# Attention with the denominators' product from summed key tiles, four buffers of probabilities, and half of the value projection moved ahead of the first values

## The chip, the cores and the metric

One core of a Trainium2 chip runs one program. The metric is the device time of one execution in microseconds, lower is better.

## The reference

The input is 16 sequences of 256 tokens with 256 channels, float32. Three stages are added to it in turn: half of a mixture-of-experts layer, attention, and half of the same expert layer again. Only the attention bears on this change:

```python
q = (X @ Wq).reshape(b, t, 16, 32).transpose(0, 2, 1, 3)     # 16 heads of 32
k, v = ...                                                    # 8 key/value heads of 32
q = q * cos + _rotate_half(q) * sin                           # the same for k
k, v = jnp.repeat(k, 2, axis=1), jnp.repeat(v, 2, axis=1)
att = 50.0 * jnp.tanh(einsum('bhqd,bhkd->bhqk', q, k) * 256.0 ** -0.5 / 50.0)
att = jnp.where(causal, att, -jnp.inf)
y = einsum('bhqk,bhkd->bhqd', softmax(att), v)
return y.transpose(0, 2, 1, 3).reshape(b, t, 512) @ Wo
```

X is layer-normalised before, and the result is added to the stage's input.

## The kernel before

The program runs the first expert layer, the attention, and the second expert layer one behind the other. The attention (function `attention`) takes one sequence of 256 tokens a slot, 16 slots. Each engine has its own instruction order, written out by hand in a function `slot_of`, and the engines meet on semaphores. For sequences 1 to 12 TensorE runs a loop whose body holds two slots; the rest is written out. The slots overlap three sequences: in the slot of sequence b TensorE also works on the projections of b + 1, the transposes of b + 2 and the last values and output product of b - 1.

A sequence has two groups (g) of four key/value heads, and two tiles (t) of 128 keys; a unit u = 2g + t is one group with one key tile. For a unit:

- `score_unit` makes the transposed scores, keys in the partitions: four heads, for each the two query heads that share it. Key tile 0 has all 256 queries (512 columns a head), key tile 1 only the later 128 (256 columns a head), since the earlier ones do not see those keys.
- ScalarE makes tanh (`cap`, tile `capped`) and the exponential (`exponential`, tile `probs`), each 128x2048 or 128x1024.
- GpSimd zeroes what is above the diagonal in the first 128 queries of the unit (`causal`), in place in `probs`, and counts `probs_ready`.
- `weighted_values` makes two products, each with 4 heads, 32 output partitions a head: `den`, with weights of ones (`m.ones_f`), so that each of the 32 partitions of a head holds the sum over keys, and `pv`, with the values `v`. Both add over the two key tiles in PSUM. In float32 each call shows as two instructions in the trace, so that a bank of four heads is eight.

`probs` has two buffers, by u % 2. After both tiles of a group VectorE's `invert` transposes `den` (32x32 blocks), takes reciprocals of one column of each block and transposes back, ScalarE's `take_values` copies `pv` to SBUF, and `divide` multiplies the two to `y`. `output` multiplies `y` with Wo into the bank `pj[0]`, and `residual` adds it to the input. `project(b, q, n)` has four pieces: n = 0 to 2 are chunks of queries and keys, which VectorE's `turn` reads (product with cos, and a shuffle to `turned`) and GpSimd's `rope` finishes (product with sin, sum); n = 3 is the value projection, copied by ScalarE (`copy_v`). Each piece is 12 matmuls of 256 columns, in a split of high and low parts (`split_matmul`). `PIECE_BANK = (1, 0, 0, 1)`: piece 3 goes into the bank that piece 0 had, so it waits for the first turn. `aT_lo_part` and `aT_hi_part` make the low and high part of the transposed input that the projections read; GpSimd's `root` and VectorE's `statistics` belong to the layer norm of b + 2.

GpSimd's order in a slot is causal 0, rope, causal 1, rope, root, causal 2, rope, causal 3.

Of the kernel before, what the change touches and what calls it, by code (L numbers as in the profile page):

```python
# [18 lines left out]
P = 128  # L19
# [1265 lines left out]
def attention(nc, m, src, dst, front):  # L1285

    ctx = ExitStack()
    with ctx:
# [35 lines left out]
        probs = sb("probs", [P, 2, JH, W], F32)  # L1324
# [33 lines left out]
        pv_done = sem("pv_done")  # L1358
        taken = sem("taken")
# [39 lines left out]
        def _(pe):  # L1399
# [9 lines left out]
            def project(b, q, n):  # L1409
# [7 lines left out]
                for c in range(2):  # L1417
# [9 lines left out]
                last.then_inc(piece_ready, 1)  # L1427
# [15 lines left out]
            def weighted_values(b, q, u):  # L1443
                g, t = u // QT, u % QT
                pe.wait_ge(probs_ready, b * UNITS + u + 1)
                if t == 0:
                    at_least(pe, taken, b * GROUPS + g)
                    at_least(pe, den_taken, b * GROUPS + g)
                n = REP * (SEQ - t * P)
                for bank, ones in ((den, True), (pv, False)):  # L1450
                    for j in range(JH):
                        w = m.ones_f[:] if ones else v[:, q, t, (JH * g + j) * HD:(JH * g + j + 1) * HD]
                        out = bank[j * HD:(j + 1) * HD, :].rearrange("p (r s) -> p r s", r=REP)[:, :, t * P:SEQ]
                        last = nc.tensor.matmul(out, w, probs[:, u % 2, j, 0:n].rearrange("p (r s) -> p r s", r=REP),  # L1454
                                                start=t == 0, stop=t == QT - 1)
                last.then_inc(pv_done, 1)
# [13 lines left out]
            def slot_of(b, q, behind=True, ahead=True, further=True):  # L1470

                score_unit(b, q, 0)
                if behind:
                    weighted_values(b - 1, 1 - q, 3)
                if ahead:
                    project(b + 1, 1 - q, 0)
                    project(b + 1, 1 - q, 1)
                score_unit(b, q, 1)
                weighted_values(b, q, 0)
                score_unit(b, q, 2)  # L1480
                if ahead:
                    project(b + 1, 1 - q, 2)
                    project(b + 1, 1 - q, 3)
                weighted_values(b, q, 1)
                score_unit(b, q, 3)
                if behind:
                    output(b - 1)
                weighted_values(b, q, 2)
# [14 lines left out]
            weighted_values(SEQS - 1, 1, 3)  # L1503
            output(SEQS - 1)

        @block.scalar
        def _(act):
# [25 lines left out]
            def exponential(b, u):  # L1533

                act.wait_ge(capped_ready, b * UNITS + u + 1)
                at_least(act, pv_done, b * UNITS + max(u - 1, 0))
                n = REP * (SEQ - u % QT * P)
                nc.scalar.activation(probs[:, u % 2, :, 0:n], capped[:, u % 2, :, 0:n], ACT.Exp,  # L1538
# [41 lines left out]
        def _(pool):  # L1580
# [17 lines left out]
            def causal(b, u):  # L1598
# [3 lines left out]
                diag = probs[:, u % 2, :, 0:n].rearrange("p j (r s) -> p j r s", r=REP)[:, :, :, 0:P]  # L1602
# [33 lines left out]
        def _(dve):  # L1636
# [26 lines left out]

            def invert(b, g):
                n = b * GROUPS + g
                dve.wait_ge(pv_done, b * UNITS + QT * (g + 1))
# [16 lines left out]
            def slot_of(b):  # L1683
# [12 lines left out]
                invert(b, 0)  # L1696
                if behind:
                    residual(b - 1)
                divide(b, 0)
                if further:  # L1700
                    aT_lo_part(b + 2)

# [96 lines left out]
```

## Time and profile before

| | |
|---|---|
| median of 3 runs | 1027.0 us (1026.89 to 1028.26) |
| the profiled execution's own time | 1027.73 us |
| its span | 1026.0 us |
| attention in the span, first scores to last residual | 366.5 to 695.1 us |
| one slot in the steady part | 20.23 us |
| TensorE's granted clock over the span | 0.979 of full speed |

The span is from the first to the last instruction of the profiled execution; its own time is a little longer, and sums are made against that. Line numbers, as L1454, are lines of the kernel before. In the trace PE is TensorE, DVE VectorE, ACT ScalarE, POOL GpSimd. A row of a tile names the tile written, an arrow and the tiles read; the tiles of the attention end in _at. Line 80 to 82 is `split_matmul`, 1438 the scores, 1454 the products of `weighted_values`, 1467 `output`, 1603 `causal`, 1594 and 1596 `rope`, 1667 to 1671 `invert`, 1677 `divide`, 1662 the shuffle of `turn`.

### The profile page before, as it was taken

The page shows a single profiled execution, that of the slowest core. Times are in us where ns is not written, and L with a number is a line of the kernel's source. Part 1 is how long each engine was busy: PE and PEld are TensorE (multiplying, and loading weights), DVE is VectorE, ACT ScalarE, POOL GpSimd, SP SyncE. Part 2 cuts the span into 40 slices and gives each one's busy share as a digit, 9 for nine tenths or more (in the row PEclk, how much of TensorE's full clock was granted, in tenths as well). Part 3 has the DMA queues.
Part 4 walks back from the last instruction along what each step waited for, and adds up shares of the span by engine and source line. Part 5 has one row for each costly group of instructions (what it writes and reads, how often), then busy time and mean ns, then how long its engine had stood idle before and what let it go on. Part 6 is the DMA issues. An engine that isn't in the chain of part 4 may idle for free. (4 is left out here: it accounts for less than half of the span.)

```text
span 1026.0 us, 17887 instructions
## 1 busy us (share of the span) xinstructions
PE 939.1 (92%) x6146; PEld 694.0 (68%) x6146; DVE 626.0 (61%) x1637; ACT 521.2 (51%) x765; POOL 472.7 (46%) x534
## 2 busy tenths in 40 slices
PE   2999998999999489999999999977999989999997
PEld 1788876777778456565666556635888767777786
DVE  4888777544444456665665676545988776453435
ACT  3766742132233257776777677655676622231322
POOL 5333203556542075776577567613512224555640
PEclk9999999999999799999999999988999999999999
DMA  5434235778774300000100100013323265777835
GB/s 186 118 96 126 67 95 150 172 179 184 174 172 104 123 1 22 21 21 31 31 20 21 41 20 21 11 62 94 94 84 111 68 175 133 170 182 180 181 58 170
DMA packets 95432, 101.90 MB, mean 99 GB/s; under 512 B 18688, under 2 KB 86656, under 8 KB 95360
## 3 DMA queue, kind: packets, MB, share of 16 engines
q1 hardware_dynamic: 83072, 83.17, 27.0%
q0 software_dynamic: 12288, 17.83, 10.4%
q8 instruction: 37, 0.61, 0.2%
q14 instruction: 35, 0.29, 0.1%
HBM read 65.44 MB, written 35.54 MB: 98 GB/s over the span
## 5 line engine op out<-in xcount | busy, mean ns | idle before, releaser
L80 PE MATMUL gu<-x_hi,gu_hi 128*128 128x512 f32 x308 | 139.9, 454 | 4.8 <-DVE act_gu L1124 4.8
L82 PE MATMUL gu<-x_lo,gu_hi 128*128 128x512 f32 x308 | 123.1, 400 | 0.0
L81 PE MATMUL gu<-x_hi,gu_lo 128*128 128x512 f32 x308 | 122.5, 398 | 0.0
L1603 POOL TENSOR_SCALAR_AFFINE_SELECT probs_at<-probs_at 128x1024 f32<-128x1024 f32 x64 | 70.5, 1102 | 110.8 <-ACT probs_at L1538 110.8
L1530 ACT ACTIVATE capped_at<-scores_at 128x2048 f32<-128x2048 f32 x64 | 93.1, 1454 | 45.1 <-PE scores_at L1438 44.9
L671 POOL DMA_INDIRECT rows<-z_rows,slots x64 | 68.9, 1077 | 75.4 <-DVE slots L1115 56.5
L957 ACT CAST a_hi<-act_gu 128x512 fp32r<-128x512 f32 x96 | 59.2, 616 | 83.1 <-DVE act_gu L1124 62.2
L1538 ACT ACTIVATE probs_at<-capped_at 128x2048 f32<-128x2048 f32 x64 | 95.2, 1487 | 2.0
L80 PE MATMUL down<-down_hi,a_hi 128*128 128x256 f32 x300 | 93.7, 312 | 0.2 <-DVE a_lo L1134 0.2
L867 PE MATMUL zT<-w_gu,xT 128*128 128x352 f32 x256 | 86.3, 460 | 0.0
L1005 ACT ACTIVATE y<-gu,rows 128x256 f32<-128x256 f32 x64 | 30.3, 474 | 109.9 <-PE gu L887 95.9
L81 PE MATMUL down<-down_hi,a_lo 128*128 128x256 f32 x300 | 83.7, 279 | 0.0
L82 PE MATMUL down<-down_lo,a_hi 128*128 128x256 f32 x300 | 83.7, 279 | 0.0
L679 POOL DMA_INDIRECT acc<-y,slots x32 | 51.1, 1597 | 70.5 <-DMA acc<-y,slots 58.6
L679 POOL DMA_INDIRECT out<-y,slots x32 | 51.3, 1604 | 69.9 <-DMA out<-y,slots 55.4
L258 POOL TENSOR_TENSOR rstd_f<-var_in_f,neg_half 128x8 f32<-128x8 f32 x16 | 26.7, 1670 | 120.6 <-DVE var_in_f L253 120.6
L949 ACT ACTIVATE silu<-gu 128x512 f32<-128x512 f32 x80 | 47.6, 596 | 61.6 <-PE gu L82 58.3
L1239 DVE TENSOR_SCALAR xT<-zT,w_norm_pairs 128x128 f32<-128x128 f32 x128 | 39.0, 346 | 62.4 <-PE zT L858 47.7
L80 PEld LDWEIGHTS gu<-x_hi,gu_hi 128*128 128x128 f32 x308 | 59.0, 192 | 21.8 <-DVE act_gu L1124 6.9
L887 PE MATMUL gu<-w_down,prodT 88*128 88x256 f32 x256 | 70.7, 399 | 0.5 <-issue 0.5
L1454 PE MATMUL den_at<-probs_at,ones_f 128*32 128x256 f32 (+1 forms) x512 | 55.4, 504 | 14.8 <-POOL probs_at L1603 14.8
L1596 POOL TENSOR_TENSOR roped_at<-by_cos_at,by_sin_at 128x512 f32<-128x512 f32 x48 | 66.4, 1383 | 3.8
(220 smaller groups left out, 2403.3 us busy)
## 6 DMA issues: line engine op xcount, KB each, us to landing
w_gu<-in_w_gate SPq DMA_DIRECT2D x64, 176.0 KB
w_gu<-in_w_up SPq DMA_DIRECT2D x64, 176.0 KB
w_down<-in_w_down SPq DMA_DIRECT2D x64, 176.0 KB
z_rows<-z SPq DMA_DIRECT2D x16, 512.0 KB, 3.1
acc<-base SPq DMA_DIRECT2D x10, 512.0 KB, 3.6
out<-base SPq DMA_DIRECT2D x10, 512.0 KB, 4.0
x_f<-in_X SPq DMA_DIRECT2D x8, 512.0 KB, 4.7
xn_at<-acc SPq DMA_DIRECT2D x16, 256.0 KB, 2.8
```

Source lines behind the costliest of these rows:

```text
L80: nc.tensor.matmul(out, w_hi, x_hi, start=first, stop=False)
L81: nc.tensor.matmul(out, w_lo, x_hi, start=False, stop=False)
L82: return nc.tensor.matmul(out, w_hi, x_lo, start=False, stop=last)
L671: pool.indirect_dma_start(out=gathered_rows[:, n, :], out_offset=None, in_=m.z_rows, in_offset=bass.IndirectOffsetOnAxis(ap=slots[:, e:e + ...
L679: pool.indirect_dma_start(out=acc, out_offset=bass.IndirectOffsetOnAxis(ap=slots[:, e:e + 1], axis=0), in_=y[:, e % HELD_Y, :], in_offset= ...
L867: last = nc.tensor.matmul(gu_ps, xT[:, e % 2, k, :], w_gu[:, n, :, k, :], start=k == 0, stop=k == KC - 1)
L887: last = nc.tensor.matmul(y_ps, prodT[:, e % 2, k, :], w_down[:, n, k, :], start=k == 0, stop=k == 1)
L957: nc.scalar.copy(a_hi[rows_, mt, :], act_gu[rows_, mt % 2, :]).then_inc(a_hi_ready, 1)
L1530: nc.scalar.activation(capped[:, u % 2, :, 0:n], scores[:, :, 0:n], ACT.Tanh, scale=QK_SCALE / SOFTCAP).then_inc(capped_ready, 1)
L1538: nc.scalar.activation(probs[:, u % 2, :, 0:n], capped[:, u % 2, :, 0:n], ACT.Exp, scale=SOFTCAP).then_inc(exp_ready, 1)
L1596: pool.tensor_tensor(roped[:, q, c:c + 2, :], by_cos[:, n], by_sin[:, n], ALU.add).then_inc(roped_ready, 1)
L1603: pool.affine_select(out=diag, in_=diag, compare_op=ALU.is_ge, fill=zero, base=0, pattern=[[0, JH], [0, REP], [1, P]], channel_multiplier= ...
```

## The change

- `probs` has four buffers, one a unit. The exponential of unit u now waits for the denominators (`den_done`) of the same group one sequence earlier, where it waited for the values of the unit two before.
- The denominators leave `weighted_values`, which keeps the product with the values. A new `denominators(b, g)` on TensorE makes, for the first 128 queries, the ones product of key tile 0 alone, and for the later 128 the ones product of a tile `both`; each is 256 columns a head and neither adds in PSUM.
- A new `add_tiles(b, g)` on VectorE makes `both`: key tile 0's later 128 queries plus key tile 1, 4 heads x 2 x 128 columns, 128x1024 in float32. It waits for the masks of both units and for the denominators that read this buffer a sequence ago. `denominators` waits for it (`summed`), and `invert` for `denominators`.
- On TensorE `denominators(b - 1, 1)` stands behind the last values of b - 1, `denominators(b, 0)` between `output(b - 1)` and the third values.
- The value projection of b + 1 is cut in two halves of 128 tokens, six matmuls each; the first goes between the scores of unit 1 and the values of unit 0, the second stays.
- On VectorE `add_tiles(b, 0)` stands behind the third turn and ahead of the residual, `invert(b, 0)` moves behind the residual, then come `add_tiles(b, 1)`, `aT_lo_part(b + 2)` and, now last, `divide(b, 0)`.

```diff
--- before.py
+++ after.py
@@ -1321,7 +1321,8 @@
         roped = sb("roped", [P, 2, 6, SEQ], F32)
         v = sb("v", [P, 2, QT, C], F32)
         capped = sb("capped", [P, 2, JH, W], F32)
-        probs = sb("probs", [P, 2, JH, W], F32)
+        probs = sb("probs", [P, UNITS, JH, W], F32)
+        both = sb("both", [P, GROUPS, JH, REP, P], F32)
         pv_sb = sb("pv_sb", [P, GROUPS, W], F32)
         BLOCKS = W // HD
         den_T = sb("den_T", [P, BLOCKS, HD], F32)
@@ -1356,6 +1357,8 @@
         exp_ready = sem("exp_ready")
         probs_ready = sem("probs_ready")
         pv_done = sem("pv_done")
+        summed = sem("summed")
+        den_done = sem("den_done")
         taken = sem("taken")
         den_taken = sem("den_taken")
         inv_T_ready = sem("inv_T_ready")
@@ -1406,7 +1409,7 @@
                         last = nc.tensor.transpose(pj[0][:, k, t * P:(t + 1) * P], a[:, t, k * P:(k + 1) * P], m.ident[:])
                 last.then_inc(aT_ready, 1)
 
-            def project(b, q, n):
+            def project(b, q, n, halves=(0, 1)):
 
                 bank = pj[PIECE_BANK[n]]
                 if n == 0:
@@ -1414,7 +1417,7 @@
                     pe.wait_ge(aT_lo_ready, b + 1)
                 elif n >= 2:
                     pe.wait_ge(turned_ready, b * PIECES + (2 if n == 2 else 1))
-                for c in range(2):
+                for c in halves:
                     for k in range(KC):
                         if n < PIECES:
                             chunk = 2 * ((n - 1) % PIECES) + c
@@ -1424,7 +1427,8 @@
                             at = slice(c * P, (c + 1) * P)
                             last = split_matmul(nc, bank[:, c, :], aT_hi[:, k, at], aT_lo[:, k, at],
                                                 m.v_hi[:, k, :], m.v_lo[:, k, :], k == 0, k == KC - 1)
-                last.then_inc(piece_ready, 1)
+                if halves[-1] == 1:
+                    last.then_inc(piece_ready, 1)
 
             def score_unit(b, q, u):
                 g, t = u // QT, u % QT
@@ -1445,15 +1449,28 @@
                 pe.wait_ge(probs_ready, b * UNITS + u + 1)
                 if t == 0:
                     at_least(pe, taken, b * GROUPS + g)
-                    at_least(pe, den_taken, b * GROUPS + g)
                 n = REP * (SEQ - t * P)
-                for bank, ones in ((den, True), (pv, False)):
+                for j in range(JH):
+                    w = v[:, q, t, (JH * g + j) * HD:(JH * g + j + 1) * HD]
+                    out = pv[j * HD:(j + 1) * HD, :].rearrange("p (r s) -> p r s", r=REP)[:, :, t * P:SEQ]
+                    last = nc.tensor.matmul(out, w, probs[:, u, j, 0:n].rearrange("p (r s) -> p r s", r=REP),
+                                            start=t == 0, stop=t == QT - 1)
+                last.then_inc(pv_done, 1)
+
+            def denominators(b, g):
+
+                pe.wait_ge(summed, b * GROUPS + g + 1)
+                at_least(pe, den_taken, b * GROUPS + g)
+                for of_both in (False, True):
                     for j in range(JH):
-                        w = m.ones_f[:] if ones else v[:, q, t, (JH * g + j) * HD:(JH * g + j + 1) * HD]
-                        out = bank[j * HD:(j + 1) * HD, :].rearrange("p (r s) -> p r s", r=REP)[:, :, t * P:SEQ]
-                        last = nc.tensor.matmul(out, w, probs[:, u % 2, j, 0:n].rearrange("p (r s) -> p r s", r=REP),
-                                                start=t == 0, stop=t == QT - 1)
-                last.then_inc(pv_done, 1)
+                        if of_both:
+                            weights = both[:, g, j]
+                        else:
+                            weights = probs[:, QT * g, j].rearrange("p (r s) -> p r s", r=REP)[:, :, 0:P]
+                        at = slice(of_both * P, (of_both + 1) * P)
+                        out = den[j * HD:(j + 1) * HD, :].rearrange("p (r s) -> p r s", r=REP)[:, :, at]
+                        last = nc.tensor.matmul(out, m.ones_f[:], weights, start=True, stop=True)
+                last.then_inc(den_done, 1)
 
             def output(b):
                 pe.wait_ge(y_ready, b * GROUPS + GROUPS)
@@ -1472,19 +1489,23 @@
                 score_unit(b, q, 0)
                 if behind:
                     weighted_values(b - 1, 1 - q, 3)
+                    denominators(b - 1, 1)
                 if ahead:
                     project(b + 1, 1 - q, 0)
                     project(b + 1, 1 - q, 1)
                 score_unit(b, q, 1)
+                if ahead:
+                    project(b + 1, 1 - q, 3, (0,))
                 weighted_values(b, q, 0)
                 score_unit(b, q, 2)
                 if ahead:
                     project(b + 1, 1 - q, 2)
-                    project(b + 1, 1 - q, 3)
+                    project(b + 1, 1 - q, 3, (1,))
                 weighted_values(b, q, 1)
                 score_unit(b, q, 3)
                 if behind:
                     output(b - 1)
+                denominators(b, 0)
                 weighted_values(b, q, 2)
                 if further:
                     transposes(b + 2)
@@ -1501,6 +1522,7 @@
             slot_of(SEQS - 2, 0, further=False)
             slot_of(SEQS - 1, 1, ahead=False, further=False)
             weighted_values(SEQS - 1, 1, 3)
+            denominators(SEQS - 1, 1)
             output(SEQS - 1)
 
         @block.scalar
@@ -1533,9 +1555,9 @@
             def exponential(b, u):
 
                 act.wait_ge(capped_ready, b * UNITS + u + 1)
-                at_least(act, pv_done, b * UNITS + max(u - 1, 0))
+                at_least(act, den_done, (b - 1) * GROUPS + u // QT + 1)
                 n = REP * (SEQ - u % QT * P)
-                nc.scalar.activation(probs[:, u % 2, :, 0:n], capped[:, u % 2, :, 0:n], ACT.Exp,
+                nc.scalar.activation(probs[:, u, :, 0:n], capped[:, u % 2, :, 0:n], ACT.Exp,
                                      scale=SOFTCAP).then_inc(exp_ready, 1)
 
             def take_values(b, g):
@@ -1599,7 +1621,7 @@
 
                 wait_apart(pool, exp_ready, b * UNITS + u + 1, pool_marks)
                 n = REP * (SEQ - u % QT * P)
-                diag = probs[:, u % 2, :, 0:n].rearrange("p j (r s) -> p j r s", r=REP)[:, :, :, 0:P]
+                diag = probs[:, u, :, 0:n].rearrange("p j (r s) -> p j r s", r=REP)[:, :, :, 0:P]
                 pool.affine_select(out=diag, in_=diag, compare_op=ALU.is_ge, fill=zero, base=0,
                                    pattern=[[0, JH], [0, REP], [1, P]], channel_multiplier=-1).then_inc(probs_ready, 1)
 
@@ -1661,9 +1683,17 @@
                 dve.tensor_tensor(by_cos[:, n], bank[:], cos, ALU.mult)
                 dve.stream_shuffle(turned[:, n], bank[:], [(i + HD // 2) % HD for i in range(HD)]).then_inc(turned_ready, 1)
 
+            def add_tiles(b, g):
+
+                dve.wait_ge(probs_ready, b * UNITS + QT * (g + 1))
+                at_least(dve, den_done, (b - 1) * GROUPS + g + 1)
+                first = probs[:, QT * g].rearrange("p j (r s) -> p j r s", r=REP)[:, :, :, P:SEQ]
+                second = probs[:, QT * g + 1, :, 0:REP * P].rearrange("p j (r s) -> p j r s", r=REP)
+                dve.tensor_tensor(both[:, g], first, second, ALU.add).then_inc(summed, 1)
+
             def invert(b, g):
                 n = b * GROUPS + g
-                dve.wait_ge(pv_done, b * UNITS + QT * (g + 1))
+                dve.wait_ge(den_done, n + 1)
                 dve.transpose(den_T[:].rearrange("p n d -> p (n d)"), den[:]).then_inc(den_taken, 1)
                 dve.wait_ge(den_taken, n + 1)
                 dve.reciprocal(inv_T[:], den_T[:, :, 0]).then_inc(inv_T_ready, 1)
@@ -1693,12 +1723,14 @@
                     statistics(b + 2)
                 if ahead:
                     turn(b + 1, 2)
-                invert(b, 0)
+                add_tiles(b, 0)
                 if behind:
                     residual(b - 1)
-                divide(b, 0)
+                invert(b, 0)
+                add_tiles(b, 1)
                 if further:
                     aT_lo_part(b + 2)
+                divide(b, 0)
 
             statistics(0)
             statistics(1)
```

## Rows read from the trace of the kernel before

**Rows 1.** Page, engines' busy time over the whole span.
```profile
PE 939.1 (92%) x6146; PEld 694.0 (68%) x6146; DVE 626.0 (61%) x1637; ACT 521.2 (51%) x765; POOL 472.7 (46%) x534
```

**Rows 2.** Windows of one slot, slot 14 and slot 15: busy us (instructions), clock, DMA.
```profile
506.24:526.47 20.23, 19.46 (x165) 12.12 (x164) 13.03 (x24) 14.86 (x14) 13.28 (x13) 1.00 0.09 26
647.68:667.13 19.45, 18.88 (x161) 11.62 (x160) 10.86 (x19) 13.88 (x12) 12.24 (x10) 1.00 0.01 4
667.13:690.60 23.47, 16.39 (x132) 6.77 (x128) 8.81 (x14) 13.08 (x11) 4.41 (x4) 0.85 0.21 66
```

**Rows 3.** TensorE in order of time, slot 7, and outputs of slot 15: start, length.
```profile
506.24 1.14 PE L1438 MATMUL scores_at<-roped_at 32*128 32x512 f32 x8
...
507.31 0.64 PE L1454 MATMUL den_at<-probs_at,ones_f 128*32 128x256 f32 x8
...
508.31 0.39 PE L80 MATMUL pj_at<-aT_hi_at,qk_hi 128*128 128x256 f32 x1
...
511.31 0.71 PE L1438 MATMUL scores_at<-roped_at 32*128 32x256 f32 x8
...
512.79 1.06 PE L1454 MATMUL den_at<-probs_at,ones_f 128*32 128x512 f32 x8 [0.77 <-POOL probs_at L1603]
...
513.64 1.07 PE L1454 MATMUL pv_at<-probs_at,v_at 128*32 128x512 f32 x8
...
514.64 1.14 PE L1438 MATMUL scores_at<-roped_at 32*128 32x512 f32 x8
...
515.71 0.38 PE L80 MATMUL pj_at<-aT_hi_at,qk_hi 128*128 128x256 f32 x1
...
518.74 0.64 PE L1454 MATMUL den_at<-probs_at,ones_f 128*32 128x256 f32 x8
...
519.19 0.61 PE L1454 MATMUL pv_at<-probs_at,v_at 128*32 128x256 f32 x8
...
519.74 0.71 PE L1438 MATMUL scores_at<-roped_at 32*128 32x256 f32 x8
...
520.38 3.72 PE L1467 MATMUL pj_at<-o,y_at 128*128 128x256 f32 x16
...
524.03 1.06 PE L1454 MATMUL den_at<-probs_at,ones_f 128*32 128x512 f32 x8
...
681.58 3.72 PE L1467 MATMUL pj_at<-o,y_at 128*128 128x256 f32 x16
...
690.62 3.72 PE L1467 MATMUL pj_at<-o,y_at 128*128 128x256 f32 x16 [2.60 <-DVE y_at L1677]
```

**Rows 4.** GpSimd in order of time: the end of slot 0, and slot 7.
```profile
384.23 1.10 POOL L1603 TENSOR_SCALAR_AFFINE_SELECT probs_at<-probs_at 128x1024 f32<-128x1024 f32 x1
...
511.44 1.10 POOL L1603 TENSOR_SCALAR_AFFINE_SELECT probs_at<-probs_at 128x1024 f32<-128x1024 f32 x1 [6.64 <-ACT probs_at L1538]
...
512.51 1.28 POOL L1594 TENSOR_TENSOR by_sin_at<-turned_at,sin 128x512 f32<-128x512 f32 x1
...
513.87 1.60 POOL L1596 TENSOR_TENSOR roped_at<-by_cos_at,by_sin_at 128x512 f32<-128x512 f32 x1
...
517.86 1.30 POOL L1596 TENSOR_TENSOR roped_at<-by_cos_at,by_sin_at 128x512 f32<-128x512 f32 x1
...
523.93 1.10 POOL L1603 TENSOR_SCALAR_AFFINE_SELECT probs_at<-probs_at 128x1024 f32<-128x1024 f32 x1
```

**Rows 5.** VectorE's groups by line and form: one with 1024 elements a partition.
```profile
L1162 DVE TENSOR_TENSOR base<-base,x_f 128x1024 f32<-128x1024 f32 x4 | 4.7, 1222 | 0.1
```

**Rows 6.** VectorE in order of time, slot 7; last row: tile y_at, all 32.
```profile
508.45 0.72 DVE L1667 STREAM_TRANSPOSE den_T_at<-den_at 128x512 f32<-128x512 f32 x1 [0.71 <-PE pv_at L1454]
...
510.70 0.74 DVE L1662 STREAM_SHUFFLE turned_at<-pj_at 128x512 f32<-128x512 f32 x1
...
512.66 1.68 DVE L1677 TENSOR_TENSOR y_at<-pv_sb_at,inv_den_at 128x512 f32<-128x512 f32 x1
...
L1677 DVE TENSOR_TENSOR y_at<-pv_sb_at,inv_den_at x32: 684/1212/1693, 381.8 to 689.9; 128x512 f32<-128x512 f32 x32
```

## The prediction

> **What bounds the kernel now.** I read the page first, then a table of windows cut at the slots, the order of time of each engine in one slot, and the groups by line. The page gives TensorE 92% of the span [rows 1]. The diff touches only the attention, 16 slots of one sequence each between 366.5 and 694 us, so the next view is one slot: 20.23 us long, TensorE's matmuls busy 19.46, at the full 2.4 GHz (granted 1.00), VectorE 13.03, ScalarE 14.86, GpSimd 13.28 [rows 2]. The reader should see that TensorE is the bound and the others have 5 to 7 us of room, but that this room is not free: each of them works in a fixed order, so the place of their idle time matters.
>
> I call the stations of TensorE's slot S0 to S3 (scores), W0 to W3 (weighted values, now with denominators), P (projections), O (output), T (transposes). Their starts [rows 3] show one wait that is not work: W0 starts at 512.79, 0.77 of it waiting for GpSimd's mask, which is only done at 512.54 [rows 4]. S1 to S2 would otherwise be free at 511.31 + 0.64 (as S3 to O) = 511.95, so the hole is 0.84 us.
>
> GpSimd is the second thing to see: it starts its first mask 5.20 us after S0 (511.44 less 506.24; scores, tanh and exponential stand in front of it) and then has no idle time until its fourth mask ends at 525.03, 18.79 after S0 [rows 3, 4]. Anything that delays it in that stretch delays the fourth mask one for one.
>
> **TensorE, work removed.** A bank of four 512-wide outputs takes 0.85 us (512.79 to 513.64), of four 256-wide ones 0.45 (518.74 to 519.19) [rows 3]. Now a group's denominators are 0.85 + 0.45; afterwards two 256-wide sets, 0.90, which is 0.40 less. By width alone it would be half of 0.85, 0.43. I take 0.85 a slot for the two groups. By place: W0 loses 0.85, W1 0.45, the stretch W3 to P0 gains 0.45 (values, then two sets), the stretch O to S0 keeps its length.
>
> **TensorE, value projection.** Six of its twelve matmuls move ahead of W0. Twenty-four take 3.00 us from 508.31 to 511.31 with the changeover to scores [rows 3], so 2.80 / 24 x 6 = 0.70 for six. They leave P2's stretch and go into the 0.84 hole. They add one changeover: a stretch of matmuls followed by another kind shows about 0.2 us beyond its streaming (3.00 against 2.80). So S1 + 0.64 + 0.90 brings W0 to 7.03 after S0, plus whatever the stretch before is late; the mask is done 6.30 after S0. The hole is gone.
> The Trainium skill (TensorEngine Tiling (Array Packing), Key Properties) says that a change of tiling mode drains the engine. By that rule the extra changeover is certain; without it the slot would be 0.2 us shorter. The 0.2 of the rows agrees.
>
> Slot without any new wait: 20.23 - 0.84 - 0.85 + 0.20 = 18.74, and laid out station by station 18.71: S0 0, W3 1.07, D1 1.52, P0 2.49, S1 5.49, half projection 6.13, W0 7.03, S2 8.03, P2 9.10, W1 11.42, S3 11.97, O 12.61, D0 16.26, W2 17.15, next S0 18.71. (D0, D1 are the denominators of the two groups.)
>
> **VectorE's adds.** One add is 128x1024 in float32 from two SBUF operands: that same size takes 1.22 us [rows 5]. Two are 2.44 a slot, VectorE 13.03 to 15.5 of about 19: not a bound by its sum. The first add follows the third turn and has until O ends; covered. Its price is on GpSimd. An SBUF-by-SBUF product of 512 takes 0.68 alone and 1.69 at most; the one issued at 512.66, while GpSimd's product ran to 513.79, ended at 514.34, 0.55 behind it, and GpSimd's next product, issued at 513.87, took 1.60 where its like takes 1.30 [rows 4, 6]. So they take turns. The third turn ends 12.2 after S0; GpSimd is then in its second rope's sum, which runs to 12.9 (519.16 less 506.24 [rows 4]). The add runs 12.87 to 13.94 and GpSimd loses 1.07 less the 0.17 by which its start is hidden in the row above, 0.90. The fourth mask ends at 18.79 + 0.90 = 19.7. If nothing is shared the loss is 0, if a blocked operation gives back nothing, 1.07 or more.
> The Trainium skill (SBUF — State Buffer, Who interferes with whom) has this rule, and it speaks against the change: a VectorE instruction with two SBUF inputs and a GpSimd one that reads SBUF exclude each other for the whole instruction. By it the slot is the 19.17 that I come to below; with a fair sharing, a loss of about 0.5, it would be 19.0. The rows above agree with the lock.
>
> **The new wait, D1.** The second add can start when the fourth mask is done (19.7) and VectorE has inverted the first group: D0 16.26, 1.14 from two 256-wide banks' start to the transpose (507.31 to 508.45 [rows 3, 6]), 1.67 for the inversion gives 19.06 and what the slot is late. So the mask decides. GpSimd is idle then, the add takes 1.22, and TensorE sees it 0.05 to 0.25 later (the mask at 512.54 let W0 go at 512.79 [rows 3, 4]): D1 may start at 21.15 after its own S0. It would start at 18.71 + 1.52 = 20.23, and with a stall s in this slot and the last, 20.23 + 2s. So s = 0.46. Behind D1 in TensorE's order stand P0, P1, S1 and all else; the stall is paid in full, once a slot. Its second effect is on the inversion and first turn behind it (2.99 us from 508.45 to the shuffle's end at 511.44 [rows 6]): turned at 5.73 + s, GpSimd wants it at 6.27; covered up to s = 0.5, beyond it each us passes on to GpSimd. The shift of aT_lo behind the add and of divide(b, 0) is hidden: P0 waits for D1 longer, and O needs y a slot later.
> The exponentials' wait moves to a denominator that is long done, and before it none of them waited for a product; four buffers give nothing by themselves. More SBUF, no DMA is touched.
>
> **Sum.** Full slot 18.71 + 0.46 = 19.17, gain 1.07. Twelve of them (2 to 13): 12.8. Slots 0 and 1 together: slot 0 loses nearly 2 us, but its fourth mask ends only at 385.33 now [rows 4] and 0.9 later with an add in front, so D1 of slot 1 waits about 2.2; I take 0.55 for both (bounds -1 and 2.5). Slot 14 has neither transposes nor root: 19.45 now [rows 2], 0.87. The last slot has no projections and waits on ScalarE; some of TensorE's work there ran at 1.2 GHz (granted 0.85 on average [rows 2]); I take it that W0 did, so that its 0.85 less is worth twice that and the last slot's first O comes 1.75 earlier, but from that O to the last one are 9.04 us now (681.58 to 690.62 [rows 3]) and then O 3.65, D0 and inversion 2.80, add 1.3, D1 and inversion 2.80, divide 0.74: 11.3. Loss 0.5. 12.8 + 0.55 + 0.87 - 0.5 = 13.7. Against the profiled execution's own 1027.73: 1014.0; the median of the runs shown is 0.73 lower, so 1013.3. The expert stage behind is the same work, started earlier; I expect nothing from it.
>
> **Rivals.**
> - The adds cost GpSimd nothing (1008 to 1010). Then the D0 chain decides: add from 19.06 + s, D1 at 20.4 + s against 20.23 + 2s, s about 0.2; gain 1.3 x 12 + 1 + 1 - 0.5 = 17, 1010; with no stall at all 1.52 a slot, 1007. For it: whichever engine issues first wins, and the second rope could be through. Against: GpSimd has no gap after its first mask. Chance 0.2.
> - GpSimd sets the pace (1017 to 1022): adds block or are blocked at more places, as when the product behind the second turn also falls on a rope, and D1 is ready at 21.7: beyond s = 0.5 the lateness feeds back, 2s = 1.47 + s - 0.49, s = 0.98, gain 0.55 x 12 = 6.6, 1020. Chance 0.18.
> - The other side: the add, whose first operand is read in eight pieces, takes 2.4 us instead of 1.22. It holds GpSimd 1.2 longer and itself ends 1.2 later; D1 is ready at 23.55, s = 3.32 - 0.49 = 2.8, slot 21.5, 1.3 longer than now: about 1043. It decides from D1 ready at 22.25, that is adds of 1.77 us each. For it: so little is needed. Against: products of equal size keep 1.22 with several shapes. Chance 0.07.
> - It does nothing that can be measured (within 0.2%): stall and saving meet, adds near 1.75. Chance 0.05.
>
> **How the numbers follow.** The forecast, 1013.3 with its own range 1010 to 1017, has 0.5. For 8 in 10 I reach to the no-stall bound and to the paced case: 1006 to 1020. Within 0.2% of no change is about what a measurement of this kernel can tell. Faster 0.88, same 0.05, slower 0.07.
>
> **What would show it.** Slot length 19.2; no wait of W0 for GpSimd; D1's weight load waiting for VectorE about 0.5 us, every slot; the first add at 1.4 to 2 us, the second at 1.22; GpSimd's first rank-root operation about 0.9 later than now; fourth mask 19.7 after S0; denominators' matmuls all 256 wide. Wrong if the first add runs clear of GpSimd, if an add is over 1.7 us with GpSimd idle, or if W0 waits again.

## The result, and the profile after

The changed kernel takes 1016.8 us (median of 4 runs, 1015.4 to 1018.5) where the kernel before takes 1027.0 (1026.9 to 1028.3): ratio 0.990, 95% interval [0.988, 0.992]. That is faster by 10.2 us; 1013.3 was forecast, and the range was 1006 to 1020. The profiled execution is the fastest of the four, 1015.36 us with a span of 1013.6.

The page's line of busy time:

```profile
PE 929.7 (92%) x6146; PEld 692.1 (68%) x6146; DVE 649.0 (64%) x1669; ACT 518.0 (51%) x765; POOL 485.5 (48%) x534
```

TensorE is still at 92% of a shorter span, with 9.4 us less of matmuls; VectorE has 23 us more [rows 1]. The adds alone are more than that (24 in slots 2 to 13 at 1.37 us on average); the product to `y`, moved to another place in the order, fell from 1.27 to 0.76 us on average in the same slots. Windows cut at slots 7, 8, 14 and 15 (columns as in [rows 2]):

```profile
500.74:520.16 19.42, 18.94 (x165) 12.02 (x165) 13.40 (x27) 14.67 (x14) 14.59 (x14) 1.00 0.08 27
520.16:539.27 19.11, 18.95 (x166) 12.01 (x165) 14.84 (x27) 14.66 (x14) 14.06 (x14) 1.00 0.09 28
635.56:654.03 18.47, 18.34 (x161) 11.57 (x160) 12.16 (x20) 13.67 (x12) 12.88 (x11) 1.00 0.01 4
654.03:677.47 23.44, 15.25 (x140) 6.69 (x136) 13.33 (x21) 13.08 (x11) 4.55 (x5) 0.88 0.21 66
```

A full slot was 20.23 and is now 19.42 or 19.11, in turn. TensorE's idle time in it is 0.5 and 0.2 us where it was 0.8. From the last slot's first scores to the last output's start are 23.44 us where they were 23.49.

TensorE in order of time in slot 7 (502.93 and 522.03 are the second group's denominators, 507.58 the half projection), and the last output:

```profile
500.74 1.14 PE L1442 MATMUL scores_at<-roped_at 32*128 32x512 f32 x8
...
501.81 0.64 PE L1456 MATMUL pv_at<-probs_at,v_at 128*32 128x256 f32 x8
...
502.93 0.64 PE L1472 MATMUL den_at<-probs_at,ones_f 128*32 128x256 f32 x8 [0.48 <-DVE both_at L1692]
...
503.93 0.39 PE L80 MATMUL pj_at<-aT_hi_at,qk_hi 128*128 128x256 f32 x1
...
506.93 0.71 PE L1442 MATMUL scores_at<-roped_at 32*128 32x256 f32 x8
...
507.58 0.39 PE L80 MATMUL pj_at<-v_hi,aT_hi_at 128*128 128x256 f32 x1
...
508.48 1.06 PE L1456 MATMUL pv_at<-probs_at,v_at 128*32 128x512 f32 x8
...
509.48 1.14 PE L1442 MATMUL scores_at<-roped_at 32*128 32x512 f32 x8
...
512.85 0.64 PE L1456 MATMUL pv_at<-probs_at,v_at 128*32 128x256 f32 x8
...
514.06 3.72 PE L1484 MATMUL pj_at<-o,y_at 128*128 128x256 f32 x16
...
517.71 0.64 PE L1472 MATMUL den_at<-probs_at,ones_f 128*32 128x256 f32 x8
...
518.17 0.61 PE L1472 MATMUL den_at<-both_at,ones_f 128*32 128x256 f32 x8
...
520.16 1.14 PE L1442 MATMUL scores_at<-roped_at 32*128 32x512 f32 x8
...
522.03 0.64 PE L1472 MATMUL den_at<-probs_at,ones_f 128*32 128x256 f32 x8 [0.16 <-DVE both_at L1692]
...
677.47 5.87 PE L1484 MATMUL pj_at<-o,y_at 128*128 128x256 f32 x16 [2.60 <-DVE y_at L1707]
```

Against [rows 3]: the first values no longer wait (508.48, 7.74 after the first scores, with no releaser behind the row), all denominators are 256 wide, and a new wait of 0.48 us stands before 502.93, for VectorE's add. GpSimd and VectorE in the same slot, in order of time:

```profile
506.02 1.11 POOL L1625 TENSOR_SCALAR_AFFINE_SELECT probs_at<-probs_at 128x1024 f32<-128x1024 f32 x1 [4.49 <-ACT probs_at L1560]
...
512.54 1.29 POOL L1618 TENSOR_TENSOR roped_at<-by_cos_at,by_sin_at 128x512 f32<-128x512 f32 x1
...
513.51 1.40 DVE L1692 TENSOR_TENSOR both_at<-probs_at 128x1024 f32<-128x1024 f32 x1
...
513.80 1.69 POOL L1606 TENSOR_TENSOR rstd_at<-var_in_at,neg_half 128x2 f32<-128x2 f32 x1
...
519.62 1.10 POOL L1625 TENSOR_SCALAR_AFFINE_SELECT probs_at<-probs_at 128x1024 f32<-128x1024 f32 x1
...
520.75 1.23 DVE L1692 TENSOR_TENSOR both_at<-probs_at 128x1024 f32<-128x1024 f32 x1
```

The reader should see the first add and GpSimd's power operation as one event. The add is issued at 513.51 beside a rope's sum that runs to 513.83; it ends at 514.91, 1.08 behind that sum. The power operation is issued at 513.80 and takes 1.69 us, 0.98 more than the 0.71 that it has when the add is thin (thin_add_0 below). The fourth mask ends at 520.72, 19.98 after the first scores, where it was 18.79 [rows 4]; VectorE's second add starts 0.03 later. The adds of the whole attention (duration ns min/median/max):

```profile
L1692 DVE TENSOR_TENSOR both_at<-probs_at x32: 1183/1226/2250, 378.0 to 672.6; 128x1024 f32<-128x1024 f32 x32
```

### The profile page after: what moved, and what is told of

Read it like the earlier page. It is cut to its first block and busy times, and to the rows that moved or that the text cites. A ratio compares the mean times of both kernels' runs of the same rounds, so it can differ in the third digit from the quotient of the medians.

```text
span 1013.6 us, 17966 instructions
## 1 busy us (share of the span) xinstructions
PE 929.7 (92%) x6146; PEld 692.1 (68%) x6146; DVE 649.0 (64%) x1669; ACT 518.0 (51%) x765; POOL 485.5 (48%) x534
## 5 line engine op out<-in xcount | busy, mean ns | idle before, releaser
L81 PEld LDWEIGHTS gu<-x_hi,gu_lo 128*128 128x128 f32 x308 | 58.9, 191 | 12.7
```

What stands on the lines that cost most here:

```text
L81: nc.tensor.matmul(out, w_lo, x_hi, start=False, stop=False)
```

## The experiments

Slot lengths below are means over slots 2 to 13, from first scores to first scores. Before the change it is 20.22, in the changed kernel 19.24. Each ratio is to the kernel before as timed beside that run: its median was 1026.5 us for the first four experiments, 1024.9 for the last one, later_whole, and 1027.4 for the others.

**whole_projection.** The changed kernel without the split.

```diff
                 score_unit(b, q, 1)
-                if ahead:
-                    project(b + 1, 1 - q, 3, (0,))
                 weighted_values(b, q, 0)
...
-                    project(b + 1, 1 - q, 3, (1,))
+                    project(b + 1, 1 - q, 3)
```

> The changed kernel with the value projection again in one piece behind the second scores. Theory (the stall ahead of the second group's denominators sets the slot, and it shifts the first values behind the mask by itself): the slot stays at 19.0 to 19.3, 1013 to 1018, nothing measurable against the changed kernel; the first values wait for the mask again, 0.2 to 0.5 us, and the stall of the denominators alternates around 0.5. Rival (the filled hole is a gain of its own, 0.64 a slot): 19.9 a slot, 1025.

Measured: 1018.8 us, ratio to the kernel before 0.992 [0.990, 0.994]; slot 19.31, alternately 19.05 and 19.6. Its TensorE, in order of time:

```profile
502.67 1.14 PE L1442 MATMUL scores_at<-roped_at 32*128 32x512 f32 x8
...
504.92 0.64 PE L1472 MATMUL den_at<-probs_at,ones_f 128*32 128x256 f32 x8 [0.54 <-DVE both_at L1690]
...
508.94 0.71 PE L1442 MATMUL scores_at<-roped_at 32*128 32x256 f32 x8
...
509.58 1.07 PE L1456 MATMUL pv_at<-probs_at,v_at 128*32 128x512 f32 x8
...
510.87 0.71 PE L1442 MATMUL scores_at<-roped_at 32*128 32x512 f32 x4 [0.22 <-ACT capped_at L1550]
```

The first values start 6.91 after the first scores with no wait for the mask in this slot: the denominators' wait (0.54 idle) and the longer stretch before the projections have moved them past the mask by themselves. The scores behind them (510.87) wait 0.22 for a tanh instead. In the shorter slots between, the first values do wait for the mask, but about 0.1 us and not the 0.2 to 0.5 expected. By the slots the split is worth 0.07 each, 1 us in all; the intervals of the two ratios overlap. The theory held in the main (the slot is just above its 19.0 to 19.3, the time 0.8 us above its range); the rival's 1025 is excluded.

GpSimd loses the same microsecond here in another place. In the shorter slots the add is issued ahead of the rope's sum (533.98, 1.22 us), that sum then takes 2.31 us (534.02) for 1.30, the power operation is back at 0.71, and the fourth mask still ends 19.90 after the slot's first scores (522.30).

**half_projection.** The kernel before with the split alone.

```diff
...
+                if ahead:
+                    project(b + 1, 1 - q, 3, (0,))
                 weighted_values(b, q, 0)
...
-                    project(b + 1, 1 - q, 3)
+                    project(b + 1, 1 - q, 3, (1,))
```

> The kernel before with only the value projection cut in two, the first half ahead of the first values. Theory (there the hole of 0.84 us is real and nothing else is late): 0.70 of work goes into it, 0.2 of changeover is added, slot 19.6, gain 0.64 x 13 = 8 us, 1018 to 1020. Rival (the mask is shifted along with it, or TensorE is held elsewhere): 20.2 a slot, 1026.

Measured: 1018.1 us, ratio 0.992 [0.991, 0.994]; slot 19.59, each one 19.58 or 19.59. TensorE in order of time, scores, half projection and first denominators:

```profile
540.29 1.14 PE L1439 MATMUL scores_at<-roped_at 32*128 32x512 f32 x8
...
546.00 0.39 PE L80 MATMUL pj_at<-v_hi,aT_hi_at 128*128 128x256 f32 x1
...
546.91 1.06 PE L1455 MATMUL den_at<-probs_at,ones_f 128*32 128x512 f32 x8
```

The half goes into the hole (546.00 to 546.91, 0.91 with its changeover), and nothing else is late. Alone it is worth 0.63 a slot, 8 us. So either part alone gives some 8 us and both together 10: they are paid from the same hole. In slots, where the last output's length plays no part, it is 0.63 for the split, 0.91 for the rest (whole_projection) and 0.98 for both.

**thin_add_0, thin_add_1.** One of the two adds covers 8 elements a partition instead of 1024.

```diff
+            dve.memset(both[:], 1.0)
             statistics(0)
...
-                dve.tensor_tensor(both[:, g], first, second, ALU.add).then_inc(summed, 1)
+                at = slice(0, 1 if g == 0 else P)
+                dve.tensor_tensor(both[:, g, :, :, at], first[:, :, :, at], second[:, :, :, at], ALU.add
+                                  ).then_inc(summed, 1)
```

(thin_add_1 has `g == 1`.) The sums that a thin add leaves out stay at one, so that group's denominators for the later queries are not the real ones; TensorE's work is the same.

> The changed kernel, but the first group's add covers one query column in 128 (8 elements a partition instead of 1024); the tile is set to ones once, so the first group's denominators of the later queries are not the real ones. Theory (the add takes 0.9 to 1.0 us from GpSimd in each slot, half of which returns as the wait for the second group's denominators): GpSimd's power operation back from 1.69 to 0.71 us, fourth mask 18.9 after the slot's first scores, slot 18.95, 4 us less than the changed kernel, 1012 to 1014. Rival (GpSimd loses nothing that matters): 19.25 a slot, 1016 to 1017.

Measured: 1011.1 us, ratio 0.986 [0.984, 0.988]; slot 18.88. GpSimd's power operation and fourth mask, in the slot whose first scores are at 516.12:

```profile
529.09 0.71 POOL L1606 TENSOR_TENSOR rstd_at<-var_in_at,neg_half 128x2 f32<-128x2 f32 x1
...
533.90 1.10 POOL L1625 TENSOR_SCALAR_AFFINE_SELECT probs_at<-probs_at 128x1024 f32<-128x1024 f32 x1
```

The operation is back at 0.71, and the mask ends 18.88 after the scores, 1.1 earlier than in the changed kernel. VectorE's own busy time fell by only 0.36 us a slot (14.44 to 14.08; the thin add still takes 0.75 to 0.86, as it is issued while the rope's sum runs), at a place with 2.9 us of idle time behind it in the changed kernel: the 0.36 by which the slot is shorter came through GpSimd. Half of 0.9 to 1.0 had been said. It is less because the mask no longer decides: the second add now starts 19.2 to 19.3 us after the first scores, right behind VectorE's inversion of the first group, where the mask is done at 18.88. The second group's denominators start 20.52 after their slot's first scores (516.12 to 536.64), in place of 21.29.

> The changed kernel, but the second group's add covers one query column in 128, the tile set to ones once (second group's denominators of the later queries not the real ones). Theory (this add and the mask ahead of it are what the denominators wait for): no wait, slot 18.7 to 18.75, 13 x 0.5 = 7 us less than the changed kernel, 1009 to 1011, and no alternation between slots. Rival (VectorE's or TensorE's order holds the slot at 19.2 whatever the add costs): 1016 to 1017.

Measured: 1011.0 us, ratio 0.985 [0.982, 0.987]; slot 18.80, alternately 18.73 and 18.87. TensorE in order of time, last values of two neighbouring slots (first scores 499.56 and 518.44) and denominators:

```profile
500.75 0.64 PE L1456 MATMUL pv_at<-probs_at,v_at 128*32 128x256 f32 x8
...
519.51 0.64 PE L1456 MATMUL pv_at<-probs_at,v_at 128*32 128x256 f32 x8
...
519.96 0.61 PE L1472 MATMUL den_at<-probs_at,ones_f 128*32 128x256 f32 x8
```

The denominators' wait is gone, they start 0.45 behind the values. GpSimd's power operation is still at 1.69 here, and that is almost free, but not quite: the last values need the fourth mask. They start 1.19 after the first scores at 499.56, 0.05 behind the end of the mask (499.60 and 1.10 long), and 1.07, their own place, after those at 518.44. This hand-over too reaches into the next slot, and so the delay of 0.12 comes in every second slot: that is the small alternation, against the expectation.

**adds_twice.** Both adds made twice, the first time into a spare tile.

```diff
+                dve.tensor_tensor(spare[:, g], first, second, ALU.add)
                 dve.tensor_tensor(both[:, g], first, second, ALU.add).then_inc(summed, 1)
```

> The changed kernel with each add made twice, the first time into a spare tile, so 2.45 us in place of 1.22 for each group. Theory (both adds stand in the chain mask, add, denominators, and once the stall is beyond 0.5 us it comes back through the turned tile and GpSimd): slot 21.3 to 21.6, stall near 2.8 us, slower than before the change, 1042 to 1048. Rival (each add costs only its own length on VectorE, which has 2 us of idle time left): 19.3 to 19.6 a slot, 1017 to 1021; or only once, without the feedback: 20.4, 1032.

Measured: 1039.1 us, ratio 1.012 [1.010, 1.014]; 20.6 to 20.7 a slot, one of 22.3, mean 20.81. In the one of 22.3 (from 511.48) TensorE's granted clock was 0.62 on average from 515.98 to 520.53, and the projections there took 4.55 us, where they take 3.0; without that slot the mean is 20.68. The side was right, the size too high. GpSimd, VectorE and TensorE in the slot of 554.35:

```profile
562.02 1.28 POOL L1617 TENSOR_TENSOR by_sin_at<-turned_at,sin 128x512 f32<-128x512 f32 x1 [1.29 <-DVE turned_at L1685]
...
568.66 1.70 POOL L1607 TENSOR_TENSOR rstd_at<-var_in_at,neg_half 128x2 f32<-128x2 f32 x1
...
569.72 1.21 DVE L1694 TENSOR_TENSOR both_at<-probs_at 128x1024 f32<-128x1024 f32 x1
...
570.35 0.67 POOL L1608 TENSOR_SCALAR back_at<-moments_at 128x2 f32<-128x2 f32 x1
...
578.48 0.64 PE L1473 MATMUL den_at<-probs_at,ones_f 128*32 128x256 f32 x8 [1.73 <-DVE both_at L1694]
```

GpSimd's first rope product waits for the turned tile (562.02, idle 1.29 before it), as the feedback had it. But the doubled add's second instruction (569.72) and the power operation ran side by side, and only the next small operation lost 0.45; the double add took 1.4 us from GpSimd, where 2.1 had been counted. With that the sum is 18.79 + 0.08 + 1.4 + 1.29 + 2.5 = 24.06, and the denominators start 24.13 after the slot's first scores.

**four_buffers.** The kernel before with `probs` of four buffers (`u` for `u % 2` at each use), the exponential waiting for `pv_done` of its own unit a sequence earlier.

```diff
...
-        probs = sb("probs", [P, 2, JH, W], F32)
+        probs = sb("probs", [P, UNITS, JH, W], F32)
...
-                at_least(act, pv_done, b * UNITS + max(u - 1, 0))
+                at_least(act, pv_done, (b - 1) * UNITS + u + 1)
```

> The kernel before with four buffers of probabilities and nothing else; each exponential waits for the values of its own unit one sequence earlier. Theory (no exponential waited for a buffer): slot 20.23, time that of the kernel before within 0.2%, 1025 to 1028. Rival (the buffers let the mask come earlier and so shorten the wait of the first values): up to 0.8 a slot, 1016 to 1024.

Measured: 1027.1 us, ratio 1.000 [0.998, 1.001], slot 20.23. The buffers alone give nothing.

**later_denominators.** The second group's denominators ahead of the next slot's first values.

```diff
                     weighted_values(b - 1, 1 - q, 3)
-                    denominators(b - 1, 1)
...
                     project(b + 1, 1 - q, 3, (0,))
+                if behind:
+                    denominators(b - 1, 1)
                 weighted_values(b, q, 0)
...
-                if behind:
-                    invert(b - 1, 1)
                 if ahead:
                     turn(b + 1, 0)
                     turn(b + 1, 1)
-                if behind:
-                    divide(b - 1, 1)
                 if further:
                     statistics(b + 2)
+                if behind:
+                    invert(b - 1, 1)
+                    divide(b - 1, 1)
...
-                add_tiles(b, 1)
                 if further:
                     aT_lo_part(b + 2)
+                add_tiles(b, 1)
                 divide(b, 0)
```

> The changed kernel with the second group's denominators moved from behind their last values to ahead of the next slot's first values, and VectorE's order with it (low part ahead of the second add; the two turns and the statistics ahead of the second group's inversion). The adds cost what they did. Theory (only the place of the wait matters): no wait, every slot 18.7 to 18.8, no alternation, 1009 to 1011 although GpSimd still loses its 1 us a slot. Rival (GpSimd, which the add lengthens, paces the slot): 19.2, 1016 to 1017.

Measured: 1008.8 us, ratio 0.983 [0.981, 0.985]; slot 18.84, alternately about 18.78 and 18.90. GpSimd's power operation and fourth mask of the slot before, and TensorE's first scores, last values, denominators and first values:

```profile
567.49 1.69 POOL L1607 TENSOR_TENSOR rstd_at<-var_in_at,neg_half 128x2 f32<-128x2 f32 x1
...
573.24 1.14 PE L1442 MATMUL scores_at<-roped_at 32*128 32x512 f32 x8
...
573.30 1.09 POOL L1626 TENSOR_SCALAR_AFFINE_SELECT probs_at<-probs_at 128x1024 f32<-128x1024 f32 x1
...
574.44 0.64 PE L1456 MATMUL pv_at<-probs_at,v_at 128*32 128x256 f32 x8
...
579.59 0.64 PE L1472 MATMUL den_at<-probs_at,ones_f 128*32 128x256 f32 x8
...
580.48 1.04 PE L1456 MATMUL pv_at<-probs_at,v_at 128*32 128x512 f32 x8
```

The denominators wait for nothing any more, and GpSimd still loses its 0.98. It was mostly the place of the wait that cost, not the add. But a small wait is left, as in thin_add_1: the last values (574.44) start 0.05 behind the end of the fourth mask, 1.20 after the first scores where 1.07 is their place, and 1.13 after them in the slot before (554.45 to 555.58). These delays, 0.13 and 0.06 in turn, are 0.09 on average, and with the 18.75 of a slot without a stall that is the 18.84 measured. So moving the consumer gave back 0.40 of the changed kernel's 0.49, GpSimd's loss keeps the rest, and "no wait, no alternation" did not come true.

**later_and_tail.** As above, and for the last group both key tiles go through TensorE with no add, the first ahead of the fourth mask.

```diff
...
+            def last_denominators(t):
...
+                for j in range(JH):
...
+                    last = nc.tensor.matmul(out, m.ones_f[:], probs[:, QT + t, j, 0:n].rearrange("p (r s) -> p r s", r=REP),
+                                            start=t == 0, stop=t == QT - 1)
...
+            last_denominators(0)
             weighted_values(SEQS - 1, 1, 3)
-            denominators(SEQS - 1, 1)
+            last_denominators(1)
...
+                if b < SEQS - 1:
+                    add_tiles(b, 1)
```

> As later_denominators, and in the last slot the second group's denominators are made as before the change, both key tiles through TensorE with no add, the first tile ahead of the fourth mask. Theory: the last output starts 1.0 to 1.4 us earlier, counted from the last slot's first scores, 1 to 3 us less than later_denominators, 1006 to 1010. Rival (the last slot is bound by ScalarE and the mask alone): the same time as later_denominators.

Measured: 1005.8 us, ratio 0.979 [0.977, 0.981]. The last denominators and the last output:

```profile
665.57 1.07 PE L1481 MATMUL den_at<-probs_at,ones_f 128*32 128x512 f32 x8
...
666.89 0.61 PE L1481 MATMUL den_at<-probs_at,ones_f 128*32 128x256 f32 x8
...
670.10 3.72 PE L1495 MATMUL pj_at<-o,y_at 128*128 128x256 f32 x16 [2.60 <-DVE y_at L1720]
```

The last output starts 21.21 after the last slot's first scores (648.89), where it was 22.49 in later_denominators (648.01 to 670.50): 1.28 earlier. In this execution it also ran at 2.4 GHz (3.72 us, for 5.41 in later_denominators), which is part of the 3.0 us between the two medians if it did so in the others.

**later_whole.** later_and_tail with the value projection in one piece again (the diff of whole_projection).

> later_and_tail with the value projection in one piece again. Theory (the denominators now stand in the time in which the first values would wait for the mask, so that the hole has only one filler's worth of room): first values 6.5 us after the first scores in place of 7.24, the projection's 0.70 paid later, slot 18.8 to 18.9, 1004 to 1008, within 2 us of later_and_tail. Rival (the split is worth its 0.64 a slot wherever nothing stalls, as in half_projection): 19.5 a slot, 1013 to 1015.

Measured: 1004.6 us, ratio 0.979 [0.977, 0.982]; slot 18.91, in the loop 18.90 to 18.94. TensorE:

```profile
575.39 1.14 PE L1442 MATMUL scores_at<-roped_at 32*128 32x512 f32 x8
...
580.71 0.64 PE L1472 MATMUL den_at<-probs_at,ones_f 128*32 128x256 f32 x8
...
581.91 1.06 PE L1456 MATMUL pv_at<-probs_at,v_at 128*32 128x512 f32 x8
```

The first values start 6.52 after the first scores, about 0.13 behind the end of the mask, for which they wait; the split gives 0.07 a slot (18.84 against 18.91), and no difference in time can be told. The simpler order is as good: the denominators alone fill the hole. These last two are the best versions, by their ratios some 21 us faster than before the change and 11 faster than the change.

## Why the prediction was right

The mechanism was right: GpSimd's loss at the first add, the chain from the fourth mask over the second add to the denominators, and the stall that this leaves. The time came out 3.5 us above the forecast of 1013.3, inside the range; the gain in the profiled execution was 12.4 us for the 13.7 of the sum, and some of its terms came out by luck (below).

**The slot.** The forecast slot was 19.17, and 19.24 was measured. Its terms: without a stall 18.71 was laid out, and the two slots less their stalls give 18.75 (19.42 - 0.67 and 19.11 - 0.35, where the stall is the denominators' start less 1.52 behind the first scores: 2.19 and 1.87). The denominators were to be ready 21.15 after their slot's first scores; it was 21.29 (500.74 to 522.03). The fourth mask came 19.98 after them, 0.28 later than the 19.7 forecast; 0.08 of that is there when the first mask starts (5.28 against 5.20), 0.07 is a later first rope, 0.04 stands in small differences up to the power operation, and the loss there was 0.98 for 0.90. On the other side TensorE followed the add after 0.05 us (522.03) or 0.13 (502.93), not 0.2. The forecast had the first turned tile 5.73 + s after the first scores; its own rows give 1.52 + 1.14 + 2.99 = 5.65 + s, and 5.66 + s was measured (6.33 at s = 0.67). GpSimd wants the tile at about 6.3, so the feedback begins only at a stall above 0.6, a slip that changes nothing at 0.51.

**The alternation** was not forecast, though the equation had it. Denominators ready at X after a slot's first scores mean that this slot's stall and the next one's add up to X - 20.27, with 18.75 for the slot: 1.02 here. The sum is fixed, the single stall is not; 0.67 and 0.35 follow each other through the whole loop. The mean, 0.51, stands against the 0.46 of the forecast. It follows too that the mean slot lies halfway between 18.75 and X - 1.52: as long as the denominators wait, only half of what is saved on TensorE or on the way to X shortens the slot.

**The hole.** The prediction credited the hole's 0.84 to the moved projection. Whole_projection and half_projection show that this part of the working is only half the story: the credit is due once, and the denominators' longer stretch and the stall claim it too. The sum is unharmed, since all was laid out in one slot, but as an account of which edit brings what it misleads: 8 us and 8 us make 10.

**GpSimd's share.** The step that the first add costs GpSimd 0.90, and that half of this comes back as stall, held: the loss was 0.98, and thin_add_0 took away 0.36 a slot. It is not a full half, because without the loss the denominators are ready at 20.52, set by the first group's inversion: the two stalls then add up to 0.25 in place of 1.02, and 18.75 + 0.12 is the 18.88 measured. That chain is the one of the first rival, which took s to be 0.2.

By the Trainium skill (SBUF — State Buffer, Who interferes with whom) a VectorE instruction with two SBUF inputs and a GpSimd one that reads SBUF exclude each other. The trace agrees for the first add, which ends 1.08 behind the rope's sum, and for the power operation's 1.69; adds_twice bounds it: beside the rest of the power operation the next add ran unhindered, 1.21 us.

**The rivals.** Free adds (1008 to 1010) are excluded by the 1.69. That GpSimd paces the slot (1017 to 1022) is excluded by the mean of 19.24, though the time, 1016.8, comes close to it by other losses. The rival on the other side was real in kind: adds of 2.45 us made the kernel 12 us slower than before, in the direction and through the feedback forecast, at 20.7 a slot and not 21.5; the mis-sized term is GpSimd's loss, 1.4 for 2.1.

**What the sum missed.** In the profiled executions: slots 0 and 1 gave 0.50 (0.55 forecast; 38.06 against 38.56), slots 2 to 13 11.7 (12.8; the slot is 0.07 longer than forecast, and slot 13 took 20.04 already before), slot 14 0.98 (0.87), the last slot to its last output's start 0.05 (-0.5).

The first of these agrees by luck, and the last looks better than it is. Slot 0 became 0.91 shorter, not nearly 2, and slot 1 became 0.40 longer, where the denominators of slot 0's second group start 1.89 late (3.41 after the first scores for 1.52) and not 2.2. In the last slot, the stretch from the first output to the last is 11.37 (666.10 to 677.47) for the 11.3 forecast, and the first output came 2.38 earlier, not 1.75. But part of this is the clock: before the change three stretches of that slot ran at 1.2 GHz (first denominators, values and third scores, 1.93, 1.94 and 1.88 us for 1.06, 1.07 and 1.14), in the changed kernel the third scores did (2.09). In four_buffers and half_projection, whose last slot has the order of before, less of it ran at 1.2 GHz: the first output started 13.63 after the first scores in both, the last 22.66. Against them the changed kernel's first output came 1.56 earlier (12.07) and its last 0.78 later (23.44).

Then comes a term that was in no step: the last output ran partly at 1.2 GHz and took 5.87 us for 3.72 [rows 3], with 2.6 us of idle time before it as before the change. From the last output's end the rest of the kernel was 1.4 us shorter in this execution. 11.0 to the end of the attention and 1.4 are the 12.4 of the spans; the medians give 10.2. What the other three executions lost was not profiled. The last output's length, in one profiled execution each, was 3.72 in the kernel before, four_buffers, thin_add_1, later_and_tail and later_whole, and 5.41 to 6.65 in the changed kernel and the five others, so a couple of microseconds of the difference between single executions is likely there; that is argued, not shown. The last slot can hold as much: in thin_add_0 it took 26.12 to the last output's start, with its first output at 5.00 us for 3.72.

## What to carry to other kernels

Lay the slot out once with every station and take the saving from the layout, not from a list of edits: two edits that fill the same hole are paid once. When work moves to an engine with idle time, ask whom it locks out at that place and who waits for the end of its own result; here the add itself was cheap, and its position just ahead of its consumer cost 0.5 us a slot, of which a later consumer gave back 0.4. Then look for the next one that waits for the same result: here the last values, 0.09 us a slot. A hand-over that reaches over one period fixes only the sum of two neighbouring stalls, so look at the mean of two slots before explaining a single one.

## What the runs showed of the hardware

- A VectorE sum of 1024 elements a partition with two SBUF operands, issued ahead of a GpSimd operation on 128x2 elements, made that operation 1.69 us long instead of 0.71; issued ahead of a GpSimd sum on 128x512, it made that one 2.31 instead of 1.30 (whole_projection). But in adds_twice the next such sum (569.72 to 570.93) ran at its undisturbed 1.21 us beside the 128x2 operation, which went on to 570.36, 0.57 us behind the end of the sum that had held it up (568.40, 1.40 us). The exclusion is thus not for all of GpSimd's 0.71.
- The last output, 16 matmul instructions behind 2.6 us of idle time, took 3.72 us in some executions and up to 6.65 in others. The kernel before and half_projection have the same order in the last slot, and it took 3.72 in one and 5.41 in the other: the order of the instructions does not fix at which of its two clock levels TensorE meets it.
